# A decoder's attention chains: scores on four row groups of 32, keys in two masked versions, norms on GpSimd, a new order

## What is computed

```
x = _layernorm(x + _L0_attn_ref(...))    # a0: linear attention over the batch, 16 heads
x = _layernorm(x + _L0_xattn_ref(...))   # x0: 16 heads, mask
x = _layernorm(x + _L0_ffn_ref(...))     # f1: two layers of local attention and a gated FFN
x = _layernorm(x + _L1_attn_ref(...))    # a1: 16 heads, no mask
x = _layernorm(x + _L1_xattn_ref(...))   # x1: 16 heads, no mask
x = _layernorm(x + _L1_ffn_ref(...))     # g, gelu: an FFN for the first half of the tokens
x = _layernorm(x + _L2_attn_ref(...))    # ema: a decaying scan
x = _layernorm(x + _L2_xattn_ref(...))   # x2: 32 heads of 4, mask
x = _layernorm(x + _L2_ffn_ref(...))     # top1: 16 experts, one chosen
x = _layernorm(x + _L3_attn_ref(...))    # a3: 16 heads, causal, relative positions
x = _layernorm(x + _L3_xattn_ref(...))   # x3: 16 heads, mask
x = _layernorm(x + _L3_ffn_ref(...))     # top2: 8 experts, two chosen
```

```
scores = jnp.einsum('bhqd,bhkd->bhqk', q, k) / scale
scores = jnp.where(mask, NEG, scores)
attn = jax.nn.softmax(scores, axis=-1)
out = jnp.einsum('bhqk,bhkd->bhqd', attn, v) @ Wo + bo
```

## Time and profile before

| | us |
|---|---|
| median of three timed runs | 927.79 (923.42 to 928.20) |
| the profiled execution, its own time | 925.06 |
| its span in the trace | 923.3 |
| TensorE busy in the span | 774.0 (84%) |
| VectorE | 588.4 (64%) |
| ScalarE | 472.5 (51%) |
| GpSimd | 353.3 (38%) |
| mean granted TensorE clock | 0.904 of full speed |

### The profile page before, as it was taken

The page is one execution under the profiler, slowest core; times in us unless marked ns, Lnnn a source line. Parts: engine busy times, 40 slices in busy tenths (PEclk is TensorE's granted clock), DMA queues, the critical chain, the costliest instruction groups (busy, mean ns, idle before and its releaser), DMA issues.

```text
span 923.3 us, 21465 instructions
## 1 busy us (share of the span) xinstructions
PE 774.0 (84%) x8139; PEld 551.1 (60%) x8139; DVE 588.4 (64%) x1573; ACT 472.5 (51%) x1094; POOL 353.3 (38%) x508
## 2 busy tenths in 40 slices
PE   5787968788998877999979997399289998899996
PEld 2465735565667765777447775155156676477665
DVE  4866958988897738988389883223178797211212
ACT  2114645677778655776337663044067574333341
POOL 3338713432444224444168750300566574000101
PEclk8877977999999998999969995689699899799999
DMA  8024000000000000000170000301745200000000
GB/s 310 1 77 174 2 2 1 1 2 1 2 1 2 1 2 1 3 3 3 39 236 3 3 3 1 88 27 35 222 136 169 65 2 3 0 1 1 1 12 12
DMA packets 31426, 37.98 MB, mean 41 GB/s; under 512 B 2912, under 2 KB 22624, under 8 KB 30816
## 3 DMA queue, kind: packets, MB, share of 16 engines
q1 hardware_dynamic: 30816, 35.58, 12.0%
q0 software_dynamic: 512, 1.05, 0.4%
HBM read 28.36 MB, written 8.26 MB: 40 GB/s over the span
## 4 chain that ended last, share of the span: by engine, by line
PE 48%; DVE 22%; issue 8%; POOL 7%; ACT 6%; DMA 4%; SPq 1%; DVEq 0%; POOLq 0%; ACTq 0%
PE bank L965 6%; PE bank L975 6%; PE bank L752 4%; PE bank L773 4%; PE bank L761 3%; PE bank L925 3%; DVE pairs L1476 2%; PE bank L788 2%; DVE pairs L1470 2%; DMA rel_scratch<-G 2%; PE bank L842 2%; POOL sm L1733 2%; DVE sm L1423 2%; POOL rstd L1705 1%; DVE mx L1426 1%
## 5 line engine op out<-in xcount | busy, mean ns | idle before, releaser
L1704 POOL TENSOR_SCALAR veps<-mv 128x1 f32<-128x1 f32 x112 | 29.4, 263 | 250.7 <-DVE mv L1361 250.4
L1733 POOL TENSOR_TENSOR sm<-sm,mx 128x512 f32<-128x512 f32 x80 | 84.0, 1053 | 43.8 <-DVE mx L1426 43.3
L1080 ACT COPY pT<-bank 128x512 f32<-128x512 f32 x112 | 65.5, 584 | 36.7 <-PE bank L761 35.3
L1075 ACT ACTIVATE pr<-sm 128x512 f32<-128x512 f32 x112 | 70.3, 632 | 25.4 <-POOL sm L1733 23.8
L761 PE MATMUL bank<-W,pr 128*128 128x128 f32 x448 | 72.5, 286 | 9.2 <-ACT pT L1080 7.3
L1643 DVE SCALAR_TENSOR_TENSOR XB<-bank,QM,XB 128x128 f32<-128x128 f32 x64 | 18.0, 344 | 92.3 <-PE bank L975 92.3
L1728 POOL TENSOR_TENSOR pairs<-KS,quad 128x512 f32<-128x512 f32 x56 | 60.0, 1073 | 27.8 <-ACT KS L1057 27.6
L752 PE MATMUL bank<-pairs,Q 64*128 64x256 f32 x448 | 68.6, 427 | 2.1 <-DVE sm L1411 1.0
L1705 POOL TENSOR_TENSOR rstd<-veps,W 128x1 f32<-128x1 f32 x112 | 64.2, 573 | 9.3
L773 PEld LDWEIGHTS bank<-VX,pT 64*64 64x64 f32 x3584 | 59.8, 139 | 11.9 <-issue 6.0
L965 PE MATMUL bank<-XT,big 128*128 128x512 f32 x128 | 64.2, 628 | 2.2 <-ACT G L1219 2.2
(11 more groups left out here) (292 smaller groups left out, 1879.9 us busy)
## 6 DMA issues: line engine op xcount, KB each, us to landing
big<-gup SPq DMA_DIRECT2D x4, 1024.0 KB, 8.8
rel_scratch<-G SPq DMA_DIRECT2D x16, 256.0 KB, 2.9
W<-small SPq DMA_DIRECT2D x1, 3206.5 KB, 12.0
big<-early SPq DMA_DIRECT2D x2, 1557.0 KB, 8.4
big<-down SPq DMA_DIRECT2D x8, 256.0 KB, 8.6
big<-e3w SPq DMA_DIRECT2D x2, 1024.0 KB
big<-e3w SPq DMA_DIRECT2D x8, 256.0 KB
QM<-rel_scratch SPq DMA_DIRECT2D x16, 128.0 KB, 2.7
```

Source lines behind the costliest of these rows:

```text
L1075: act.activation(pr[:, u % 2, 4 * h:4 * h + 4, :, :].rearrange("p g b k -> p b g k"), sm[:, 2 * (u % 2) + h, :].rearrange("p (b g k) -> p ...
L1080: act.copy(pT[:, u % 2, 4 * h:4 * h + 4, :], bank[BK[f"tu{h}"]][:, :].rearrange("p (h n) -> p h n", h=4)).then_inc(pt_ready, 1)
L1733: tt(v, v, bc(mx[:, slot, :], [P, 8, S], 2), ALU.subtract).then_inc(pcentered, 1)
```

## The change

- **Scores.** `sc` is now eight matmuls: sequence b by row group r of four, each 32 rows (4 heads) by 128 moving columns, with the same 128 stationary columns. Group r goes to the first half of bank r; banks 0 to 3 serve. The semaphore `scored` still rises twice a step, after groups 1 and 3 of the second sequence.
- **Keys.** GpSimd's product makes two masked versions, not four (128x256 elements a step). The masks `quad16` and `quad32` and the permuted weights `mixed` of x2 are built for the new layout.
- **VectorE's reading of scores.** Each half is now read as two half banks in one instruction (the PSUM banks became one tensor); in a3 the addition of the relative part is two instructions of 256 elements for one of 512.
- **Exponential.** It writes its output in the order in which it reads.
- **Norm.** The chains' `fi` moves from VectorE to GpSimd, as one tensor_scalar with two pointer scalars; its waits move with it, and VectorE counts the norm's semaphore ahead (`norm_ahead`). The norms of the last stage, top2, stay on VectorE.
- **Order.** New assumed durations, ranks, stage rank (7 to 5), patience (0.02 to 0.1), hop times, ring depths, and a new bank for nearly every kind of tile.

```diff
-CHAIN_BANK = {"k": 4, "v": 2, "q": 4, "tu0": 3, "tu1": 3, "va0": 6, "va1": 2, "fo": 5, "y": 7, "x": 5, "in": 2, "up0":
-              7, "up1": 3, "dn": 4}
...
-STAGE_RANK, CHAIN_PATIENCE = 7, 0.02
-SCORE_BANKS = (0, 1)
+CHAIN_BANK = {"k": 4, "v": 6, "q": 5, "tu0": 7, "tu1": 5, "va0": 1, "va1": 4, "fo": 0, "y": 7, "x": 5, "in": 1, "up0":
+              6, "up1": 2, "dn": 3}
+CHAIN_RANK = {"pe.sc": -3.0, "pe.v": 3.0, "pe.y": 1.5, "act.pt": 3.0, "act.k": -3.5, "pe.x": 3.0, "pe.q": -3.5,
...
+STAGE_RANK, CHAIN_PATIENCE = 5, 0.1
+SCORE_BANKS = (0, 1, 2, 3)
...
-                   ("pool.rs", 0, ["dve.re"]), ("dve.fi", 0, ["pool.rs"]), ("pe.x", 0, ["dve.fi"]), ("act.x", 0, ["pe.x"])]
+                   ("pool.rs", 0, ["dve.re"]), ("pool.fi", 0, ["pool.rs"]), ("pe.x", 0, ["pool.fi"]), ("act.x", 0, ["pe.x"])]
...
-            return pairs[:, 0:4, (u % 4) * P:(u % 4 + 1) * P]
+            return pairs[:, 0:2, (u % 4) * P:(u % 4 + 1) * P]
...
                         for b in range(2):
-                            for r in range(2):
-                                rows = slice(r * S, (r + 1) * S)
-                                last = mm(ps[r][:, b * 256:(b + 1) * 256].rearrange("p (g k) -> p g k", g=4),
+                            for r in range(4):
+                                rows = slice(r * 32, (r + 1) * 32)
+                                last = mm(bank[r][:, 0:256].rearrange("p (g b k) -> p g b k", g=2, b=2)[:, :, b, :],
                                           Q[rows, q2 + b, :, :].rearrange("p c q -> p (c q)"),
                                           keys(u)[rows, :, b * S:(b + 1) * S], start=True, stop=True)
-                                if b == 1:
+                                if b == 1 and r % 2 == 1:
                                     last.then_inc(scored, 1)
...
-                        act.activation(pr[:, u % 2, 4 * h:4 * h + 4, :, :].rearrange("p g b k -> p b g k"),
-                                       sm[:, 2 * (u % 2) + h, :].rearrange("p (b g k) -> p b g k", b=2, g=4),
+                        act.activation(pr[:, u % 2, 4 * h:4 * h + 4, :, :].rearrange("p g b k -> p (g b k)"),
+                                       sm[:, 2 * (u % 2) + h, :],
...
-                            sc = bank[b][:, :].rearrange("p (h k) -> p h k", h=8)
+                            sc = psum[:, 2 * b:2 * b + 2, 0:256]
...
-                    if step == "fi":
-                        if name == "gelu" and t >= NT:
-                            dve.wait_ge(xt_ready, xt_at[t])
-                        finish(X[:, t, :] if name == "gelu" and t >= NT else res[:, t % 4, :], t)
...
-                        quad = quad16[:, :] if name != "x2" else quad32[:, 4 * s_:4 * s_ + 4]
-                        tt(keys(u), bc(KS[:, u % 4, :], [P, 4, P], 1), bc(quad, [P, 4, P], 2), ALU.mult).then_inc(k_split, 1)
+                        quad = quad16[:, :] if name != "x2" else quad32[:, 2 * s_:2 * s_ + 2]
+                        tt(keys(u), bc(KS[:, u % 4, :], [P, 2, P], 1), bc(quad, [P, 2, P], 2), ALU.mult).then_inc(k_split, 1)
...
+                    if step == "fi":
+                        src = X[:, t, :] if name == "gelu" and t >= NT else res[:, t % 4, :]
...
+                        pool.wait_ge(rstd_ready, rstd_at[t % 4])
+                        ts(X[:, t, :], src, mv[:, t % 4, 0:1], rstd[:, t % 4, :], ALU.subtract, ALU.mult).then_inc(x_ready, 1)
```

More of the change, by code:

```diff
@@ L251, in chain_plan @@
     for step, other, *depth in CHAIN_RINGS:
-        for x2 in (0, 1) if step in ("pe.v", "pe.va") else (None,):
+        for x2 in (0, 1) if step == "pe.v" else (None,):
             mine = [j for j in queue.get(step, []) if x2 is None or (stages[j[1]] == "x2") == x2]
-            past = queue.get({"ema.y": "pe.y", "a3.sc": "dve.sc"}.get(other, other), [])
+            past = queue.get({"ema.y": "pe.y", "att.y": "pe.y", "a3.sc": "dve.sc"}.get(other, other), [])
             past = [j for j in past if x2 is None or (stages[j[1]] == "x2") == x2]
+            if other == "att.y":
+                past = [j for j in past if stages[j[1]] in ATT]
             if other in ("ema.y", "a3.sc"):
@@ L261, in chain_plan @@
             for j in mine:
-                n += 1 if step == "pe.tu" and j[4] == 0 or step != "pe.tu" and not (step == "pe.va" and x2 and j[3]) else 0
+                n += 1 if step == "pe.tu" and j[4] == 0 or step != "pe.tu" and not (step == "pe.va" and j[3]) else 0
                 if 0 <= n - depth[x2 or 0] < len(past):
@@ L305, in chain_plan @@
             free[engine] = end[key]
-        if what in ("sc", "tu") and engine == "pe":
-            freed = (CHAIN_FREES[what], key[1], key[2], key[3], 1 if what == "sc" else key[4])
+        if what == "tu" and engine == "pe":
+            freed = (CHAIN_FREES[what], *key[1:])
         else:
@@ L310, in chain_plan @@
         for b in banks(*key):
-            held[b] = freed
+            held[b] = ("dve.sc", key[1], key[2], key[3], int(b > 1)) if q == "pe.sc" else freed
         name = stages[key[1]]
@@ L460, in decoder @@
         w2_w = room(4096, 4096, "p (e c n) -> p e c n", e=NE3, c=4)
-        bank = [ctx.enter_context(nc.psum_tensor(f"bank{i}", [P, 512], F32)) for i in range(8)]
+        psum = ctx.enter_context(nc.psum_tensor("psum", [P, 8, 512], F32))
+        bank = [psum[:, i, :] for i in range(8)]
         first_in, rest_in, masks_in, f0_in, f1_in, g_in, e2_in, e3_in, wo_in = (sem(n) for n in (
@@ L1415, in chain @@
                                     dve.wait_ge(rel_back[(2 * t + c) % 4], 32 * ((2 * t + c) // 4 + 1))
-                                tt(sm[:, slot, :].rearrange("p (b n) -> p b n", b=2),
-                                   bank[b][:, :].rearrange("p (b n) -> p b n", b=2),
-                                   RBs[t % 2][:, :, b * 256:(b + 1) * 256], ALU.add).then_inc(rel_added, 1)
+                                pairs_of = lambda v, n: v.rearrange("p (g b k) -> p g b k", g=n, b=2)
+                                for r in range(2):
+                                    last = tt(pairs_of(sm[:, slot, r * 256:(r + 1) * 256], 2), pairs_of(sc[:, r, :], 2),
+                                              RBs[t % 2][:, :, (2 * b + r) * P:(2 * b + r + 1) * P].rearrange(
+                                                  "p b (g k) -> p g b k", g=2), ALU.add)
+                                last.then_inc(rel_added, 1)
                                 dve.wait_ge(rel_added, due(rel_added))
@@ L1421, in chain @@
                             else:
[L1422 to L1424 removed]
+                                own = CAPS[a["mask"]][:, 2 * t:2 * t + 2, :].rearrange("p b k -> p (b k)")
+                                two = lambda v: v.rearrange("p r (g n) -> p r g n", g=2)
+                                tt(two(sm[:, slot, :].rearrange("p (r n) -> p r n", r=2)), two(sc),
+                                   own.unsqueeze(1).unsqueeze(1).to_broadcast([P, 2, 2, P]), ALU.min).then_inc(capped, 1)
                                 dve.wait_ge(capped, due(capped))
```

71 lines of the change are left out of this document (44 added, 27 removed).

## The result

The changed kernel is slower: 966.72 us median (962.62 to 970.22) against 928.0 us for the kernel before beside it. The ratio is 1.0404, 95% interval 1.0364 to 1.0443. I had said 914, with 897 to 931 as range.

What follows compares the result with a forecast made beforehand. TensorE was taken as the bound, VectorE close behind. The terms -12.1 - 5.5 + 1.8 + 3 + 1 - 1.2 + 1 + 0 = -12.0 us turned 925.06 into 913.1 (915.8 by the timed median); forecast 914, range 897 to 931.

Steps and rivals of the forecast that it cites:

- Part 6: Scores in banks 0 to 3, shared with other tiles, and a new order: 0, ends +12 and -13 us.
- Part 1: Score steps on four row groups: 0.75 us for 1.06 each, 12.1 us gained (ends 6.3 and 18.0).
- Part 2: Chain norms taken off VectorE: 5.5 us gained (ends 0 and 10.1).
- part 3: Chain norms on GpSimd at 0.62 us each: costs 1.8 us at joints, 3 in x0, 1.0 from queueing.
- Part 4: GpSimd's key products in two versions: 0.65 us for 1.073 each; 1.2 us gained in x3, x0 counted elsewhere.
- part 5: Small edits: a3's split addition costs about 1 us on the path; score reads and exponential 0.
- The banks take the gain: Rival: TensorE waits about 0.2 us more each score step for banks; +12 us, total 926; chance 0.14.
- GpSimd becomes the bound: Rival: in x0, x2, a3, x3 the norm queues behind centrings or key products; net +9, 934 us; chance 0.10.
- Four groups don't run abreast: Rival: score row groups run two at a time; +4.7 us in place of -12.1, total 930; chance 0.06.
- The clock: Rival: less TensorE work in x0 and at joints prolongs 1.2 GHz; about 5 us given back, 919; chance 0.05.
- my main case: The prediction's own case for the whole kernel: 905 to 922 us, chance 0.48.

Runs made afterwards that it cites:

- the doubled run: The changed kernel with each score step's 16 passes issued twice: 979.71 us, ratio 1.0529 to the kernel before.
- the short norm: The changed kernel, order kept, with the chains' GpSimd norm taken over 16 of 128 features: 952.94 us, ratio 1.0232.
- stand-ins for the same savings and costs in the old order and banks: The kernel before with halved score columns and key products, and chain norms on GpSimd behind their rstd: 938.26 us, ratio 0.9951.
- The run with the four waits: New order and banks on the kernel before, halved score columns, TensorE awaiting the last readers of banks 0 to 3 before each score step: 986.71 us, ratio 1.0561.

## Why the prediction was wrong, step by step

**Part 6, banks and order: the step that failed.** I wrote "The trace of before can't price it: I take 0, with +12 and -13 as ends". It measured +42 us (1.0408 to 1.0499) by itself, three and a half times my upper end. The end was reached from a wait of 0.2 us a step, as if an order could only add small waits to a path that stays TensorE's. It can put another engine on the path: ScalarE's two copies and the key copy between the turns and the values. In the steady stretch the same instructions then take 5.72 us a step for 5.00, and with the shorter score step still 5.31. TensorE's 22.8 us more of busy time for the same passes had no term either. Most of the 42 us is ranks (3.5%); what the banks add isn't shown.

**Part 1, scores.** Right, and for the stated reason. The step is 0.66 for my 0.75. The estimate from the Trainium skill's 3.07 times was 0.73; the trace is below both. Sixteen passes more took 0.44 us in the doubled run, and my 16 x 0.112 / 4 is 0.45: four groups do run abreast, and some 0.22 us comes on top, not 0.15. The worth of shorter steps in the old order, with the key product, was 1.65% or 15.3 us (9.1 to 21.6, by the interval of the ratio); mine were 12.1, 1.2 and, in x0, 2.1, together 15.4. That the two agree so closely is partly luck: with the 0.41 us that the step really saves, my way of reckoning gives 19.4. What I left out is that the share of the path, 70%, belongs to the order and isn't kept when the order changes: in the new one the same cut showed no gain.

**Part 2 and part 3, the norm.** The terms of the move without its keys (-5.5, +1.8, +5.0, +1.0) sum to +2.3; measured +8.1 (3.5 to 12.6) in the old order. Two sizes were off. The instruction takes 0.82 us for my 0.62: it has one pointer and one operation more than L1719, and they weren't free. That is 88 x 0.2 = 18 us more GpSimd work, and by the short norm about half of such time is on the path in the changed order. And TensorE's wait for X, for which I had added 1.0 us, rose by 14 in the old order and by 10 in the changed kernel, between my 1 and the 22 that I had named for the worst. How the 5.8 us between 2.3 and 8.1 divide between them and a gain on VectorE that may have been smaller isn't shown. I also gave GpSimd's free share as 36 to 56%; in 440:470 it is 61%.

**Part 4 and part 5.** Key product 0.62 for 0.65. The two additions of a3 take 0.42 us each (0.425 assumed).

**The rivals.** "The banks take the gain" had a mechanism that is in the trace: TensorE now stands 9.9 us ahead of L760, 5.3 of them for VectorE's `on`, where it stood 2.1 ahead of L752. But that is 8 us, and ranks without the new banks did most of the damage. "GpSimd becomes the bound" had a right mechanism (its norm's length is on the path) but isn't the main cause: in the old order the move costs 8 us of the 39, and taking it out of the changed kernel, with a new plan, made that slower. "Four groups don't run abreast" is refuted by 0.66 us. The clock I had priced as 5 us given back in x0 and at joints, inside my main case. I undersized it: the mean went from 0.904 to 0.855, and in the new order the saved score time went with a fall from 0.884 to 0.854. In the old order the same cut left it at 0.896. It isn't the whole loss, as the order alone lost 42 us at 0.884; how much of the 39 us it makes, and whether it is a cause or follows from the order, the runs don't separate.

**How the parts make 4.0%.** In steps, each with its own run: order and banks 1.0454; on top of it four-group scores and two key versions 1.0614; on top of that the norm on GpSimd, with the plan that goes with it, 1.0404. They don't add up as separate terms, since each step also feeds the planner.

**What stays open.** With orders chosen anew, the changed mechanics stay at 1.0157 (1.0080 to 1.0235), while stand-ins for the same savings and costs in the old order and banks are at 0.9951 by two executions and at 1.0076 by all ten. What lies between, 1 to 2%, if it is there at all, is either that four of eight banks are held by the scores, or the 32-row passes and the clock they are granted, or an order that I didn't find. The run with the four waits was to tell and didn't. No version was faster than the kernel before with all of its computation.

## What to carry to other kernels

A share of the critical path is a property of one order. When a change remakes the order, price the parts in the old order, and give the order itself a range as wide as reordering alone has been seen to move the time; here that was 3.5 to 5.5% between runs that differ in ranks, far above the 1.7% of the best part. If it can be tried, put the mechanical change in the old order first: it separates the two at once. And where TensorE already waits, less work for it may come back as a lower clock; look at the granted clock beside the busy time before booking a saving.

## What the runs showed of the hardware

- Sixteen passes of 32 rows by 128 columns with a 128-column load each, four row groups in turn into four banks, took 0.66 us at a granted clock of 1.00 and 1.21 at 0.50. Thirty-two took 1.10, so sixteen more cost 0.44 us, 28 ns a pass, a quarter of the 112 ns of a full-array pass of 128 columns.
- GpSimd's tensor_scalar on 128x128 took 0.62 us with one pointer scalar and one operation, 0.82 with two and two, and 0.46 on 16 elements: 3.2 ns an element, (820 - 463) / 112, and 0.41 us fixed.
- In the new order, a cut of TensorE's work left its busy time as it was (796.8 to 795.9 us) while the mean granted clock fell from 0.884 to 0.854; doubling the score passes of the changed kernel raised it from 0.855 to 0.874. In the old order the same cut took the busy time from 774.0 to 761.2 us, with the clock at 0.896 for 0.904.
